# Column and row tiles for the fifth mixing input, two-pass scaled rows and a new order in a software-pipelined RWKV kernel

## The chip, the cores and the metric

The kernel runs on one core of one Trainium2 chip. The metric is the device time of one execution in microseconds, lower is better. A core has TensorE (PE, with its weight loads shown as PEld), VectorE (DVE), ScalarE (ACT), GpSimd (POOL) and SyncE (SP, which issues DMAs here). Each engine works through its own list in order, and they meet only in semaphores.

## The reference, cut to what matters

Input x is 2 x 4096 x 256, f32. It is an adaLN block: `h = layernorm(x) * (1 + ca) + sa`, then `x = x + ga * rwkv(h)`, then `h = layernorm(x) * (1 + cb) + sb` and `x = x + gb * ffn(h)`. The six modulation rows come from a small product and are one row of 256 for each batch.

rwkv has two layers and a last layernorm (`ln_out`). A layer is a time mixing and a channel mixing. What the change touches of the time mixing:

```python
sx  = shift(x) - x                              # x is the layer's layernorm
mix = tanh((x + sx * x_maa) @ tm_w1)            # 256 -> 160 = 5 groups of 32
m_f = mix[:, f] @ tm_w2[f]                      # five products 32 -> 256: w, k, v, r, g
f_x = x + sx * (f_maa + m_f)                    # then x @ Wr, Wk, Wv, Wg, and the decay from the w input
```

A recurrence over time (state times decay plus k v), a group norm, a gate and `@ Wo` follow. The ffn quantizes its input, its hidden values and its weights to blockwise FP4 (blocks of 16) and is `silu(gate) * up` with 704 hidden values, then a product down.

## The kernel before, in words

The 4096 tokens are cut into 32 tiles of 128, and both batches of a tile (NC = 2) are worked together, so a tile is 256 tokens: 128 partitions x 512 values (2 batches x 256 features) token-first, or the same with features on partitions.

The work of a tile is cut into five streams: 0 and 1 are the time mixings of layers 0 and 1 (stream 0 also holds the input layernorm), 2 and 3 the channel mixings, 4 the output layernorm and the ffn. A stream is a list of stages (`schedule`). `ORDER` gives for each engine one turn of the pipeline: `0/1 mf.2 mf.4` means stages mf.2 and mf.4 of stream 0 for the tile one turn back. Every engine runs its turn again and again, over 32 tiles and four more turns to drain; stages of tiles that do not exist are left out. Semaphores carry the dependences.

The stages that matter here:

- `lna` makes the layernorm's statistics on DVE (two bn_stats, two bn_aggr, one add), and POOL makes `rstd` of them (L562). `lnb` normalizes in two DVE tensor_scalar passes, subtract mean and multiply by rstd (L886). Seven layernorms run for a tile: in, tm0, cm0, tm1, cm1, out and ffn.
- `h0`, `x2` and `hf` follow the in, out and ffn layernorms: DVE multiplies by a modulation row in one 128x512 pass (L891), then POOL adds the shift row or the residual (L566, L628, L632).
- `turn` transposes rows to columns on PE (L1077), ACT moves them to hT (L684, L687), POOL makes sx (L572).
- `mix`: DVE makes the input (L906), PE multiplies by tm_w1: 128 columns into one half of a PSUM bank (L1109), the last 32 columns over all 256 tokens into the other (L1111); ACT takes tanh of both (L694, L695).
- `mf.0` to `mf.4`: five products of 32 rows (L1122), DVE adds maa and multiplies by sx (L918, two passes each), POOL adds x (L585). mf.0 to mf.3 read partitions 0 to 127 of the first tanh by quarters, mf.4 reads partitions 96 to 127 of the second, with the weights tm_w2b there.
- `pw1` (L1130), `pk`, `pr`, `pg` (L1085), `pv`, `wo` (L1093), `pw2` (L1164) are projections; ACT makes the decay of pw2 (L727, L731), and POOL multiplies it up over six levels (`tot`, L593).
- `lev.1` to `lev.6`: PE makes scores in small tiles (L1183, L1190), DVE scales r and k (L952) and merges scores under a mask (L954, L959). Each level's products on PE wait until DVE has emptied the previous level's two banks.
- `kt`, `st`, `ov`, `gna`, `gnb`, `yt`: transposes, states, outputs, group norm and gate. `ck`, `cr`, `cv` (L1267, L1093, L1281) are the channel mixing, `xt`, `gu`, `ht`, `dn` (L1077, L1300, L1311, L1319) the ffn, `qa` and `qc` its quantizing on DVE (L394 to L419).

Streams 0 and 1 have three PSUM banks each, A, B and C (`MIX_PSUM`); streams 2 to 4 share two, used alternately in PE's order. `fill` on PE waits until the last user of each bank has emptied it.

SP works through DVE's order: at stream 0's `wo` it waits until DVE has emptied that bank and loads the next x tile into xin (L496), at `x2` it loads x again for the residual (L500), at `dn` it waits for POOL's last add and stores (L504). In the first turns some setup hangs on names of places: the FP4 quantizing of the three ffn weights on DVE (`weights_norm`, `weights_grid`), on ACT and on PE.

Of the kernel before, what the change touches and what calls it, by code (L numbers as in the profile page):

```python
# [12 lines left out]
P = 128  # L13
# [19 lines left out]
    DVE: """0/1 mix; 4/4 qa.x; 2/2 cv; 4/4 qc.x; 1/3 st.0; 0/1 mf.0 mf.1; 1/3 st.1 gna; 4/4 gu.0.0; 0/1 mf.3; 1/3 gnb; 4/4  # L33
        gu.0.1 qa.0; 0/1 mf.2 mf.4; 1/3 wo; 4/4 qc.0; 1/2 lna.tm; 3/3 lna.cm; 0/1 lev.1; 1/2 lnb.tm; 4/4 gu.1.0; 0/1 lev.2;
        3/3 lnb.cm; 4/4 gu.1.1; 1/2 mix; 0/1 lev.3; 3/3 cmix; 0/1 pg lev.4; 1/2 mf.0; 0/1 lev.5; 1/2 mf.1 mf.3; 4/4 qa.1;
        0/1 lev.6; 4/4 qc.1; 1/2 mf.2; 0/1 st.0 st.1 gna; 1/2 mf.4; 0/1 gnb; 3/3 cv; 4/4 dn; 1/2 lev.1; 0/1 wo; 2/1 lna.cm;
        1/2 lev.2; 2/1 lnb.cm; 4/3 lna.out; 1/2 lev.3; 0/0 lna.in; 2/1 cmix; 0/0 lnb.in; 1/2 pg; 0/0 h0; 1/2 lev.4; 4/3
        lnb.out; 0/0 lna.tm; 4/3 x2; 1/2 lev.5; 0/0 lnb.tm; 4/3 lna.ffn; 1/2 lev.6; 4/3 lnb.ffn hf""",
    AC: """0/1 yt; 1/2 pv; 2/1 turn.cm; 1/2 pg; 2/1 ck.0 ck.1 ck.2 cr; 0/0 turn.tm; 1/2 kt; 4/3 qa.x; 0/0 mix; 4/3 xt; 1/2 gna;
        4/3 gu.0.0; 0/0 pw1; 4/3 gu.0.1; 0/0 pk; 1/2 yt; 4/3 qa.0; 0/0 pr pw2; 4/3 ht.0 gu.1.0; 0/0 pv; 1/1 turn.tm; 4/3  # L40
        gu.1.1; 3/2 turn.cm; 0/0 pg; 1/1 mix; 3/2 ck.0; 1/1 pw1; 4/3 qa.1; 3/2 ck.1; 1/1 pk; 0/0 kt; 3/2 ck.2 cr; 4/3 ht.1;
        1/1 pr; 0/0 gna; 1/1 pw2""",
    POOL: """3/3 cv; 1/2 mf.4; 0/1 yt; 1/2 tot; 2/1 lna.cm; 4/4 dn; 2/1 cmix; 0/0 lna.in; 4/3 lna.out; 0/0 h0 lna.tm; 4/3 x2
        lna.ffn; 0/0 mix; 4/3 hf; 1/2 st.0 st.1; 0/0 mf.0 mf.1; 1/2 gnb; 0/0 mf.3; 2/1 cv; 1/2 yt; 0/0 mf.2; 1/1 lna.tm; 3/2
        lna.cm; 0/0 mf.4 tot; 1/1 mix; 3/2 cmix; 1/1 mf.0 mf.1 mf.3; 0/0 st.0 st.1; 1/1 mf.2; 0/0 gnb""",
# [37 lines left out]
def orders(streams):  # L83
# [25 lines left out]
    "h_scaled": (["h0", "hf"], 1), "h_done": (["h0", "hf"], 1), "x2_scaled": (["x2"], 1), "x2_done": (["x2"], 1),  # L109
# [12 lines left out]
def adaln_rwkv_fp4_kernel(nc, a, out):  # L122
# [74 lines left out]
    with ExitStack() as ctx:  # L197
# [322 lines left out]
        def _(pool):  # L520
# [43 lines left out]
            def h0(i, b, _):  # L564
                after(pool, i, "h_scaled", b, "h0", 0)
                pool.tensor_tensor(xin[:, :, :], xn[b][:, :, :], rows[:, :, 0, :], ALU.add)\  # L566
                    .then_inc(ev["h_done"][b], 1)

# [55 lines left out]
            def x2_(i, b, _):  # L624
                pool.wait_ge(x_loaded_again, i * 16 + 16)
                pool.wait_ge(stored, i * 16 + 16)
                after(pool, i, "x2_scaled", b, "x2", 0)
                pool.tensor_tensor(x2[:, :, :], xagain, xn[b][:, :, :], ALU.add).then_inc(ev["x2_done"][b], 1)  # L628

            def hf(i, b, _):  # L630
                after(pool, i, "h_scaled", b, "hf", 0)
                pool.tensor_tensor(xn[b][:, :, :], xn[b][:, :, :], rows[:, :, 3, :], ALU.add)\  # L632
                    .then_inc(ev["h_done"][b], 1)
# [716 lines left out]
```

## Time and profile before

| what | value |
|---|---|
| median of 3 runs | 3316.56 us (3314.88 to 3319.21) |
| the profiled execution's own time | 3318.94 us |
| its span | 3317.2 us |
| granted TensorE clock over the span | 0.957 |
| busy: PE, PEld | 2986.0 us (90%), 2328.5 us (70%) |
| busy: DVE, POOL, ACT | 2413.7 us (73%), 1398.4 us (42%), 1269.9 us (38%) |
| DMA | 41.43 MB, mean 12 GB/s |

Busy is the time in which an engine has an instruction running; overlapping instructions count once. A clock of 1.00 is 2.4 GHz, 0.5 is 1.2 GHz. A line number names the line of the kernel that issued an instruction.

### The profile page before, as it was taken

The page shows a single profiled execution, that of the slowest core. Times are in us where ns is not written, and L with a number is a line of the kernel's source. Part 1 is how long each engine was busy: PE and PEld are TensorE (multiplying, and loading weights), DVE is VectorE, ACT ScalarE, POOL GpSimd, SP SyncE. Part 2 cuts the span into 40 slices and gives each one's busy share as a digit, 9 for nine tenths or more (in the row PEclk, how much of TensorE's full clock was granted, in tenths as well). Part 3 has the DMA queues.
Part 4 walks back from the last instruction along what each step waited for, and adds up shares of the span by engine and source line. Part 5 has one row for each costly group of instructions (what it writes and reads, how often), then busy time and mean ns, then how long its engine had stood idle before and what let it go on. Part 6 is the DMA issues. An engine that isn't in the chain of part 4 may idle for free.

```text
span 3317.2 us, 78375 instructions
## 1 busy us (share of the span) xinstructions
PE 2986.0 (90%) x32829; PEld 2328.5 (70%) x32829; DVE 2413.7 (73%) x5249; ACT 1269.9 (38%) x2451; POOL 1398.4 (42%) x1552
## 2 busy tenths in 40 slices
...
DMA packets 36212, 41.43 MB, mean 12 GB/s; under 512 B 2716, under 2 KB 34584, under 8 KB 35864
## 3 DMA queue, kind: packets, MB, share of 16 engines
...
q14 instruction: 84, 0.69, 0.1%
...
## 4 chain that ended last, share of the span: by engine, by line
PE 55%; DVE 32%; issue 5%; POOL 4%; DMA 3%; ACT 1%; SPq 0%; DVEq 0%; ACTq 0%; POOLq 0%
PE ps_all L1085 9%; PE ps_all L1267 9%; PE ps_all L1281 6%; PE ps_all L1300 5%; PE ps_all L1319 5%; PE ps_all L1093 4%; DVE stats L874 4%; DVE sxrk L952 3%; PE ps_all L1122 3%; PE ps_all L1190 3%; DMA xin<-in_L_attn_x_dram 3%; PE ps_all L1077 2%; DVE att L959 2%; DVE mixin L886 2%; DVE xn_ffn L886 2%
## 5 line engine op out<-in xcount | busy, mean ns | idle before, releaser
L585 POOL TENSOR_TENSOR mixin<-mixin,hT_tm 128x512 f32<-128x512 f32 x320 | 387.6, 1221 | 295.9 <-DVE mixin L918 295.9
L1267 PE MATMUL ps_all<-chan,cwk 128*128 128x256 f32 x1536 | 389.5, 407 | 44.4 <-DVE chan L906 44.4
L562 POOL TENSOR_TENSOR rstd<-var,powc 128x2 f32<-128x2 f32 x224 | 206.0, 922 | 503.7 <-DVE var L880 503.4
L918 DVE SCALAR_TENSOR_TENSOR mixin<-ps_all,vcol,sxrk 128x256 f32<-128x256 f32 x640 | 270.4, 477 | 192.4 <-PE ps_all L1122 191.4
L1267 PEld LDWEIGHTS ps_all<-chan,cwk 128*128 128x128 f32 x1536 | 299.5, 201 | 92.5 <-issue 48.0
L1281 PE MATMUL ps_all<-cwv,chan 128*128 128x256 f32 x1536 | 346.8, 382 | 0.5 <-ACT ffn_work L763 0.5
L1190 PEld LDWEIGHTS ps_all<-sxrk 64*64 64x64 f32 x12288 | 220.2, 136 | 175.0 <-issue 174.9
L952 DVE TENSOR_TENSOR sxrk<-sxrk,dec 128x512 f32<-128x512 f32 x384 | 271.7, 708 | 63.2 <-PE ps_all L1190 59.0
L1190 PE MATMUL ps_all<-sxrk 64*64 64x32 f32 x12288 | 258.0, 222 | 64.9 <-DVE att L959 64.7
L1281 PEld LDWEIGHTS ps_all<-cwv,chan 128*128 128x128 f32 x1536 | 287.7, 191 | 39.9 <-ACT ffn_work L763 1.1
L604 POOL TENSOR_TENSOR lora<-S,dec 128x256 f32<-128x256 f32 x128 | 84.2, 658 | 429.2 <-DVE S L967 429.1
L704 ACT ACTIVATE tok<-ps_all 128x512 f32<-128x512 f32 x128 | 76.3, 596 | 434.3 <-PE ps_all L1093 265.6
L959 DVE COPY_PREDICATED att<-masks,ps_all 128x256 f32<-128x256 uint8 x384 | 203.3, 529 | 9.7 <-DVE att L954 0.5
L1300 PE MATMUL ps_all<-gateT,ffn_work 128*128 128x352 f32 x512 | 188.8, 492 | 15.1 <-ACT ffn_work L763 14.4
L736 ACT ACTIVATE chan<-ps_all 128x512 f32<-128x512 f32 x192 | 113.9, 593 | 206.4 <-PE ps_all L1267 206.4
L1300 PE MATMUL ps_all<-upT,ffn_work 128*128 128x352 f32 x512 | 175.6, 466 | 0.0
L1319 PE MATMUL ps_all<-downT,ffn_work 128*128 128x256 f32 x768 | 173.3, 383 | 0.7 <-ACT ffn_work L767 0.7
L1319 PEld LDWEIGHTS ps_all<-downT,ffn_work 128*128 128x128 f32 x768 | 145.0, 192 | 20.0 <-ACT ffn_work L767 1.1
L1020 DVE TENSOR_TENSOR xn_ffn<-ps_all,rows 128x512 f32<-128x512 f32 x32 | 22.1, 692 | 183.5 <-PE ps_all L1319 183.5
L593 POOL TENSOR_TENSOR dec<-dec 128x256 f32<-128x256 f32 (+5 forms) x384 | 141.2, 368 | 26.5 <-ACT dec L731 1.5
L1122 PE MATMUL ps_all<-lora,tm_w2a 32*128 32x256 f32 x1024 | 146.7, 403 | 1.9 <-ACT lora L695 1.9
L609 POOL TENSOR_TENSOR grstd<-gvar,powc 128x8 f32<-128x8 f32 x64 | 105.4, 1648 | 99.7 <-DVE gvar L974 96.6
...
## 6 DMA issues: line engine op xcount, KB each, us to landing
...
```

What stands on the lines that cost most here:

```text
L562: pool.tensor_tensor(rstd[b][:, :], var[b][:, :], powc[:, 0:NC], ALU.pow).then_inc(ev["ln_rstd"][b], 1)
L585: pool.tensor_tensor(m, m, hT["tm", l][:, :, :, 1:P + 1].rearrange("p k c t -> p (k c) t"), ALU.add).then_inc(ev["mixed"][b], 1)
L918: ins = v.scalar_tensor_tensor(mixes(b, f)[:, k, :], bank(b, "mf", lf, "m")[:, k * TT:(k + 1) * TT], col(f"{MIXES[f]}_maa", l, k), sx[b][: ...
L952: v.tensor_tensor(rko, rko, t, ALU.mult).then_inc(ev["rk_lev"][b], 1)
L959: v.copy_predicated(odd, mask, data).then_inc(free_of(b, "lev", lj, "a"), 1)
L1085: ins = pe.matmul(bank(b, kind, arg, use)[:, m * TT:(m + 1) * TT], w[:, k, m * P:(m + 1) * P], x[:, k, :], start=(k == 0), stop=(k == KC - 1))
L1122: ins = pe.matmul(bank(b, "mf", lf, "m")[:, k * TT:(k + 1) * TT], w[:, k * P:(k + 1) * P], x, start=True, stop=True)
L1190: ins = pe.matmul(bank(b, "lev", lj, "a", e)[q * HH:(q + 1) * HH, n:n + HH // 2].rearrange("p (n h) -> p n h", h=half), kk[b][p, k, t], od ...
L1267: ins = pe.matmul(bank(b, "ck", lj, "k")[:, m * TT:(m + 1) * TT], cwk[:, l, k, n:n + P], k_in[:, k, :], start=(k == 0), stop=(k == KC - 1))
L1281: ins = pe.matmul(bank(b, "cv", l, "v")[:, c * D:(c + 1) * D], relu[t // 2][:, t % 2, c * P:(c + 1) * P], cwv[:, l, t, :], start=(t == 0), ...
L1300: ins = pe.matmul(bank(b, "gu", cu, use)[:, 0:IH], xqT[:, k, c * P:(c + 1) * P], w[:, k, u * IH:(u + 1) * IH], start=(k == 0), stop=(k == ...
L1319: ins = pe.matmul(bank(b, "dn", 0, "o")[:, c * D:(c + 1) * D], hqT[:, j, c * P:(c + 1) * P], downT[:, j, :], start=(j == 0), stop=(j == IT ...
```

## The change

1. The last 32 mixing columns: the product of L1111 is made for each batch by itself, 128 tokens, batch 0 into partitions 0 to 31 and batch 1 into 32 to 63, that is on two column tiles of PE. Four matmuls of 128 columns stand where two of 256 stood. Its tanh is one ACT pass of 64x128 where it was 32x256.
2. mf.4 reads these two row ranges: for each half of the features and each batch one matmul on row tile 0 or 32, each batch into a bank of its own (A and B). The weights lie in both row ranges, by one more DMA per layer. mf.4 stands ahead of mf.2 in the stream, and mf.2 uses bank C where it used A.
3. Layernorms in, out and ffn: `lnb` makes `(x - mean) * row` in two scalar_tensor_tensor passes and no longer waits for rstd; `h0`, `x2`, `hf` are two DVE scalar_tensor_tensor passes, `* rstd + shift`. The three POOL adds of 128x512 are gone, and DVE itself waits for the second load of x and for the store.
4. ORDER of all four engines is another, and so are the places of the weights' setup.

```diff
 ORDER = {
-    PE: """0/1 mf.2 mf.4; 1/3 wo; 0/1 pw2 lev.1 pv; 4/4 ht.0 gu.1.0; 0/1 lev.2; 1/2 turn.tm; 4/4 gu.1.1; 0/1 lev.3; 3/3
-        turn.cm; 0/1 pg; 1/2 mix; 0/1 lev.4; 3/3 ck.0; 1/2 mf.0 mf.1 mf.3; 0/1 lev.5; 3/3 ck.1; 0/1 lev.6; 3/3 ck.2; 1/2 pw1
-        pk pr; 0/1 kt; 3/3 cr; 1/2 mf.2 mf.4; 0/1 st.0 ov.0; 4/4 ht.1; 0/1 ov.1 st.1; 3/3 cv; 1/2 pw2; 0/1 yt; 4/4 dn; 1/2
-        lev.1; 0/1 wo; 1/2 pv lev.2 lev.3; 2/1 turn.cm; 1/2 pg lev.4; 2/1 ck.0 ck.1 ck.2; 1/2 lev.5; 2/1 cr; 1/2 lev.6; 0/0
-        turn.tm; 2/1 cv; 1/2 kt; 0/0 mix; 1/2 st.0 ov.0; 0/0 mf.0 mf.1 mf.3; 4/3 xt; 1/2 ov.1 st.1; 4/3 gu.0.0; 0/0 pw1; 4/3
-        gu.0.1; 0/0 pk; 1/2 yt; 0/0 pr""",
...
+    PE: """1/3 ov.0; 0/1 pw1; 1/3 ov.1 st.1; 2/2 cv; 1/3 yt; 0/1 pk pr; 1/3 wo; 4/4 xt; 0/1 mf.4 mf.2; 4/4 gu.0.0; 0/1 pw2
+        lev.1 pv; 3/3 turn.cm; 0/1 lev.2; 4/4 gu.0.1; 1/2 turn.tm; 0/1 lev.3 pg; 3/3 ck.0; 0/1 lev.4; 3/3 ck.1 ck.2 cr; 0/1
+        lev.5; 1/2 mix; 4/4 ht.0; 0/1 lev.6; 4/4 gu.1.0; 0/1 kt; 1/2 mf.0 mf.1 mf.3; 0/1 st.0 ov.0; 4/4 gu.1.1; 0/1 ov.1
+        st.1; 3/3 cv; 1/2 pw1; 0/1 yt; 1/2 pk pr; 0/1 wo; 1/2 mf.4 mf.2; 4/4 ht.1; 1/2 pw2; 4/4 dn; 1/2 lev.1 pv lev.2; 2/1
+        turn.cm; 0/0 turn.tm; 1/2 lev.3 pg lev.4; 2/1 ck.0 ck.1; 1/2 lev.5; 2/1 ck.2; 0/0 mix; 1/2 lev.6; 0/0 mf.0 mf.1
+        mf.3; 1/2 kt; 2/1 cr; 1/2 st.0""",
+    DVE: """4/4 gu.0.1; 0/1 lev.3; 4/4 qa.0; 0/1 pg lev.4; 1/2 mix; 4/4 qc.0; 0/1 lev.5 lev.6; 4/4 gu.1.0; 1/2 mf.0; 0/1 st.0;
+        1/2 mf.1; 4/4 gu.1.1; 1/2 mf.3; 0/1 st.1 gna; 4/4 qa.1; 0/1 gnb; 4/4 qc.1; 3/3 cv; 0/1 wo; 1/2 mf.4 mf.2; 2/1
+        lna.cm; 0/0 lna.in lnb.in; 2/1 lnb.cm; 0/0 h0 lna.tm; 1/2 lev.1; 0/0 lnb.tm; 1/2 lev.2; 4/4 dn; 1/2 lev.3; 2/1 cmix;
+        1/2 pg lev.4; 0/0 mix; 1/2 lev.5; 4/3 lna.out; 1/2 lev.6; 0/0 mf.0 mf.1; 4/3 lnb.out x2; 1/2 st.0; 0/0 mf.3; 4/3
+        lna.ffn lnb.ffn; 1/2 st.1 gna; 4/3 hf; 1/2 gnb; 4/3 qa.x qc.x; 2/1 cv; 1/2 wo; 0/0 mf.4; 3/2 lna.cm; 0/0 mf.2; 1/1
+        lna.tm; 3/2 lnb.cm; 4/3 gu.0.0; 0/0 lev.1; 1/1 lnb.tm; 0/0 lev.2; 3/2 cmix""",
+    AC: """0/1 pv; 1/2 turn.tm; 3/3 ck.0; 0/1 pg; 4/4 qa.0; 3/3 ck.1 ck.2 cr; 4/4 ht.0; 1/2 mix; 0/1 kt; 4/4 gu.1.0 gu.1.1; 0/1
+        gna; 4/4 qa.1; 0/1 yt; 1/2 pw1 pk pr; 4/4 ht.1; 1/2 pw2 pv; 2/1 turn.cm; 1/2 pg; 0/0 turn.tm; 2/1 ck.0 ck.1; 0/0
+        mix; 2/1 ck.2; 1/2 kt gna; 0/0 pw1; 2/1 cr; 1/2 yt; 4/3 qa.x; 0/0 pk pr; 4/3 xt gu.0.0; 0/0 pw2; 3/2 turn.cm; 4/3
+        gu.0.1""",
+    POOL: """1/3 yt; 2/2 cv; 0/1 mf.4; 3/3 lna.cm; 0/1 mf.2; 1/2 lna.tm; 0/1 tot; 3/3 cmix; 1/2 mix; 0/1 st.0; 1/2 mf.0; 0/1
+        st.1; 1/2 mf.1 mf.3; 0/1 gnb yt; 3/3 cv; 1/2 mf.4 mf.2; 2/1 lna.cm; 0/0 lna.in lna.tm; 1/2 tot; 2/1 cmix; 0/0 mix;
+        4/4 dn; 0/0 mf.0; 4/3 lna.out; 1/2 st.0 st.1; 4/3 lna.ffn; 0/0 mf.1; 1/2 gnb; 0/0 mf.3""",
 }
...
-            ("pk", "k"): "B", ("pr", "r"): "C", ("mf.2", "m"): "A", ("mf.4", "m"): "B", ("pw2", "w"): "BC", ("lev.1", "a"): "AB",
+            ("pk", "k"): "B", ("pr", "r"): "C", ("mf.4", "m"): "AB", ("mf.2", "m"): "C", ("pw2", "w"): "BC", ("lev.1", "a"): "AB",
...
-                act.activation(lora[b][P - E:P, 1, :], m[P - E:P, TT:2 * TT], ACT.Tanh).then_inc(free_of(b, "mix", l, "m"), 1)
+                act.activation(lora[b][0:NC * E, 1, 0:P], m[0:NC * E, TT:TT + P], ACT.Tanh).then_inc(free_of(b, "mix", l, "m"), 1)
...
                 elif at == (0, "2 cmix"):
                     weights_norm(1)
+                elif at == (0, "2 cv"):
                     weights_grid(1)
                     weights_norm(2)
+                elif at == (0, "1 lna.tm"):
                     weights_grid(2)
...
             def lnb(i, b, s):
                 src = ln_source(i, s)
+                scaled = {"in": 1, "out": 2, "ffn": 4}
+                if s in scaled:
+                    if s == "out" and i > 0:
+                        after(v, i - 1, "y_done", FFN, "dn", 0)
+                    for c in range(NC):
+                        v.scalar_tensor_tensor(xn[b][:, c, :], src[:, c, :], mv[b][:, c, 0:1], rows[:, c, scaled[s], :], ALU.subtract, ALU.mult)\
+                            .then_inc(ev["ln_xn"][b], 1)
+                    return
                 after(v, i, "ln_rstd", b, "lna", s)
...
-            def scale_rows(i, b, s, n, event):
+            def shift_rows(i, b, s, dst, shift, event):
+                after(v, i, "ln_rstd", b, "lna", s)
                 after(v, i, "ln_xn", b, "lnb", s)
-                v.tensor_tensor(xn[b][:, :, :], xn[b][:, :, :], rows[:, :, n, :], ALU.mult)\
-                    .then_inc(ev[event][b], 1)
+                for c in range(NC):
+                    v.scalar_tensor_tensor(dst[:, c, :], xn[b][:, c, :], rstd[b][:, c:c + 1], shift[:, c, :], ALU.mult, ALU.add)\
+                        .then_inc(ev[event][b], 1)
...
             def x2_(i, b, _):
-                scale_rows(i, b, "out", 2, "x2_scaled")
+                v.wait_ge(x_loaded_again, i * 16 + 16)
+                v.wait_ge(stored, i * 16 + 16)
+                shift_rows(i, b, "out", x2, xagain, "x2_done")
...
                 for k in range(KC):
-                    ins = pe.matmul(m[P - E:P, TT:2 * TT], tm_w1[:, l, k, P:P + E], mixes(b, 4)[:, k, :], start=(k == 0), stop=(k == KC - 1))
+                    for c in range(NC):
+                        ins = pe.matmul(m[c * E:(c + 1) * E, TT:TT + P], tm_w1[:, l, k, P:P + E], mixes(b, 4)[:, k, c * P:(c + 1) * P],
+                                        start=(k == 0), stop=(k == KC - 1))
...
+                    else:
+                        for c in range(NC):
+                            ins = pe.matmul(bank(b, "mf", lf, "m", c)[:, k * P:(k + 1) * P], tm_w2b[c * E:(c + 1) * E, l, k * P:(k + 1) * P],
+                                            lora[b][c * E:(c + 1) * E, 1, 0:P], start=True, stop=True)
```

On ACT, the setup's third `weights_abs` moves from behind `2 ck.2` to the head of layer 1's first `turn`. The order before of DVE, ACT and POOL is in the code above.

## Rows read from the trace of the kernel before

**Rows 1.** The page: busy time and share of the span by engine.
```profile
PE 2986.0 (90%) x32829; PEld 2328.5 (70%) x32829; DVE 2413.7 (73%) x5249; ACT 1269.9 (38%) x2451; POOL 1398.4 (42%) x1552
```

**Rows 2.** Windows: length, busy time by engine (instructions), granted clock, DMA share, GB/s.
```profile
0.00:120.00 120.00, 63.10 (x489) 43.52 (x489) 64.87 (x125) 22.98 (x39) 31.73 (x70) 0.73 0.33 101
...
500.00:1000.00 500.00, 470.45 (x5280) 367.23 (x5280) 384.40 (x842) 201.55 (x391) 224.64 (x242) 0.98 0.03 9
```

**Rows 3.** DVE's L886 and L906, steady turns: least/median/longest ns, first to last start.
```profile
L886 DVE TENSOR_SCALAR xn_ffn<-x,mv,rstd x54: 401/628/1224, 399.8 to 2922.8; 128x256 f32<-128x256 f32 x54
L906 DVE SCALAR_TENSOR_TENSOR mixin<-sxrk,vcol,hT_tm x108: 477/479/1500, 401.9 to 2959.1; 128x256 f32<-128x256 f32 x108
```

**Rows 4.** PE's timeline in one turn: start, us, operation, records [idle before, releaser].
```profile
1958.44 1.05 PE L1111 MATMUL ps_all<-mixin,tm_w 128*32 128x256 f32 x4
1959.42 0.62 PE L1218 MATMUL ps_all<-tok 64*64 64x64 f32 x13
...
1966.61 0.66 PE L1130 MATMUL ps_all<-mixin,td_w 128*64 128x128 f32 x8
1967.19 1.45 PE L1300 MATMUL ps_all<-gateT,ffn_work 128*128 128x352 f32 x4
...
1973.65 0.48 PE L1122 MATMUL ps_all<-lora,tm_w2a 32*128 32x256 f32 x1
1973.66 0.48 PE L1122 MATMUL ps_all<-lora,tm_w2b 32*128 32x256 f32 x1
...
1974.72 1.99 PE L1093 MATMUL ps_all<-wo,mixin 128*128 128x256 f32 x8
...
1978.35 0.69 PE L1183 MATMUL ps_all<-mixin,sxrk 64*64 64x64 f32 x32 [0.99 <-issue]
...
1990.23 1.89 PE L1085 MATMUL ps_all<-mixin,wg 128*128 128x256 f32 x8
```

**Rows 5.** PE's timeline about 50 us later.
```profile
2032.24 0.73 PE L1190 MATMUL ps_all<-sxrk 64*64 64x32 f32 x32 [1.61 <-DVE att L959]
...
2034.16 2.87 PE L1085 MATMUL ps_all<-mixin,wg 128*128 128x256 f32 x8
```

**Rows 6.** ACT's timeline: the decay's first passes in that turn.
```profile
1977.41 0.84 ACT L727 ACTIVATE tok<-ps_all,vcol 128x256 f32<-128x256 f32 x2 [0.72 <-PE ps_all L1164]
```

**Rows 7.** DVE's timeline: two layernorms' statistics, and a level 1 from its first pass on.
```profile
1980.08 0.74 DVE L874 BATCH_NORM_STATS2 stats<-hand 128x6 f32<-128x256 f32 x2
...
1981.33 0.74 DVE L874 BATCH_NORM_STATS2 stats<-xres 128x6 f32<-128x256 f32 x2
...
2026.52 0.70 DVE L952 TENSOR_TENSOR sxrk<-sxrk,dec 128x512 f32<-128x512 f32 x1 [0.47 <-PE ps_all L1190]
...
2028.53 0.72 DVE L987 TENSOR_TENSOR xres<-xin,ps_all 128x512 f32<-128x512 f32 x1
```

**Rows 8.** Groups by line: busy us, mean ns | idle before, releaser.
```profile
L566 POOL TENSOR_TENSOR xin<-mixin,rows 128x512 f32<-128x512 f32 x32 | 52.2, 1631 | 74.0 <-DVE mixin L891 74.0
...
L632 POOL TENSOR_TENSOR xn_ffn<-xn_ffn,rows 128x512 f32<-128x512 f32 x32 | 45.7, 1428 | 42.1 <-DVE xn_ffn L891 42.1
...
L891 DVE TENSOR_TENSOR xn_ffn<-xn_ffn,rows 128x512 f32<-128x512 f32 x64 | 44.1, 689 | 1.2
...
L628 POOL TENSOR_TENSOR x<-tok,xn_ffn 128x512 f32<-128x512 f32 x32 | 40.9, 1278 | 11.6 <-DVE xn_ffn L891 11.6
```

**Rows 9.** SP's timeline, then the landing times of L496's 31 loads.
```profile
2032.68 0.38 SPq L504 DMA_DIRECT2D out_dram<-x  x1
2033.11 0.47 SPq L496 DMA_DIRECT2D xin<-in_L_attn_x_dram  x1
...
DMA to landing us min/median/max: 2.6/2.9/4.3
```

**Rows 10.** PE's timeline in the first turns and in the last.
```profile
131.36 1.08 PE L1077 MATMUL ps_all<-ident,mixin 128*128 128x128 f32 x4 [19.21 <-DVE mixin L886]
...
3270.76 1.09 PE L1077 MATMUL ps_all<-ident,ffn_work 128*128 128x128 f32 x4 [16.07 <-DVE ffn_work L419]
```

More of the change, by code:

```diff
@@ L33 @@
[L33 to L45, printed above, removed]
+    PE: """1/3 ov.0; 0/1 pw1; 1/3 ov.1 st.1; 2/2 cv; 1/3 yt; 0/1 pk pr; 1/3 wo; 4/4 xt; 0/1 mf.4 mf.2; 4/4 gu.0.0; 0/1 pw2
[4 more added lines that the diff above has]
+        mf.3; 1/2 kt; 2/1 cr; 1/2 st.0""",
@@ L54, in schedule @@
         s += [("mf", (l, f)) for f in (0, 1, 3)]
-        s += [("pw1", l), ("pk", l), ("pr", l), ("mf", (l, 2)), ("mf", (l, 4)), ("pw2", l), ("tot", l)]
+        s += [("pw1", l), ("pk", l), ("pr", l), ("mf", (l, 4)), ("mf", (l, 2)), ("pw2", l), ("tot", l)]
         between = {1: ("pv", l), 3: ("pg", l)}
@@ L108 @@
     "ln_stats": (["lna"], 2), "ln_mv": (["lna"], 2), "ln_var": (["lna"], 1), "ln_rstd": (["lna"], 1), "ln_xn": (["lnb"], 2),
[L109 removed]
+    "h_done": (["h0", "hf"], 2), "x2_done": (["x2"], 2),
     "carried": (["turn"], 1), "shifted": (["mix", "cmix"], 1), "xxx": (["mix"], 1), "mixed": (["mf"], 1),
@@ L562, in lna @@
                 pool.tensor_tensor(rstd[b][:, :], var[b][:, :], powc[:, 0:NC], ALU.pow).then_inc(ev["ln_rstd"][b], 1)
[L564 to L567, printed above, removed]
             def shift(i, b, kind, l, stage):
@@ L622, in cv @@
                 pool.tensor_tensor(flat(hands(i, l)), flat(xres[l]), cm_r, ALU.add).then_inc(ev["cm_done"][b], 1)
[L624 to L633, printed above, removed]
             def dn(i, b, _):
@@ L637, in dn @@
                 pool.tensor_tensor(x2[:, :, :], x2[:, :, :], xn[b][:, :, :], ALU.add).then_inc(ev["y_done"][b], 1)
-            steps = {"lna": lna, "h0": h0, "mix": mix, "cmix": cmix, "mf": mf, "tot": tot, "st": st, "gnb": gnb, "yt": yt,
-                     "cv": cv, "x2": x2_, "hf": hf, "dn": dn}
+            steps = {"lna": lna, "mix": mix, "cmix": cmix, "mf": mf, "tot": tot, "st": st, "gnb": gnb, "yt": yt,
+                     "cv": cv, "dn": dn}
             turns(pool, RUN[POOL], steps, nothing)
@@ L682, in turn @@
                 h = hT[kind, l]
+                if (i, s) == (0, "tm1"):
+                    weights_abs(2)
                 filled(act, i, b, "turn", s, "x")
```

22 lines of the change are left out of this document (12 added, 10 removed).

## The prediction, on record before the changed kernel ran

> **What bounds the kernel now.** I read the page's busy shares first. PE is busy for 90% of the span, DVE for 73%, POOL and ACT for 42% and 38% [rows 1]. The windows say where the missing tenth is: in a steady window PE is busy for 470.45 of 500 us at a clock of 0.98, in the first 120 us for 63.10 at 0.73 [rows 2]. So there is a steady part, bound by PE and the waits in its list, and two ends, bound by chains of latency.
>
> The length of a steady turn comes from the first and last start of a group that runs twice a tile: 399.8 to 2922.8 us over 26 turns is 97.0 us [rows 3]. PE is busy for 94.1% of it, 91.3 us, and idle for 5.7 us. The clock's mean of 0.98 means about 2% of 97 us, 1.9 us, of full-speed work lost per turn. PE's timeline shows both. A level of batch-merged scores waits 1.61 us for DVE, and just behind it the gate's projection takes 2.87 us at the lower clock, where the same one takes 1.89 us elsewhere [rows 4, 5]. Another wait is 0.99 us before lev.1, marked "issue" [rows 4]. The code tells what it is: lev.1 uses banks A and B, pw2 used B and C, and ACT reads pw2 from 1977.41 for 0.84 us [rows 6], up to 0.1 us before lev.1 starts. The timeline's idle marks of one turn add up to 5.3 us at nine places; the largest are these two.
>
> What counts is therefore PE's work per turn, its waits in the new list, the clock, and the ends.
>
> **The fifth mixing input on PE.** Four records of 256 columns on one column tile last from 1958.44 to 1959.42, 0.98 us. The nearest row for the new form is pw1: eight records of 128 columns on two column tiles of 64, from 1966.61 to 1967.19, 0.58 us [rows 4]. Eight in a row without overlap would take 0.98 us again, so pw1 shows real overlap. I take 0.58: 0.40 saved per layer, 0.8 us per turn. Bounds: nothing saved, or 1.0 us per turn if tiles of 32 columns, with their shorter weight loads, overlap wholly. The smaller tanh (64x128 where it was 32x256) I cost at nothing; it lies on the way from mix to mf.0, 0.1 us.
>
> The Trainium skill (TensorEngine Tiling (Array Packing), Instruction Overhead) gives about 60 cycles of overhead to each matmul and advises against taking the factor from a dimension that is already small. By it the four more records cost an estimated 0.1 us per mix, some 6 us in all. The same page (Key Properties) says that changing the tiling mode drains the engine; the old product was already in a 128x32 mode, so no drain is added.
>
> **mf.4 on row tiles.** This saves PE nothing. mf.2 and mf.4 already run side by side: they start at 1973.65 and 1973.66 and both are done when wo starts at 1974.72, 1.07 us for both [rows 4]. mf.2 still has four records of 256 columns, and these fill that time. What mf.4's shorter product gives is a start for DVE about half a microsecond sooner. What it costs is banks: mf.4 holds A and B and mf.2 holds C, so pw2 (B, C) now waits for DVE's passes of both. I bound the pair by 0.9 and 1.3 us.
>
> **Rows in two DVE passes.** Before, a scaled layernorm is two tensor_scalar and one 128x512 multiply of 0.69 us, then a POOL add of 1.63, 1.28 or 1.43 us [rows 8]. The tensor_scalar passes run from 401 to 1224 ns [rows 3]. After, it is four scalar_tensor_tensor of 479 ns, 1.92 us, against 2 x 0.63 + 0.69 = 1.95 us by the medians: even on DVE, between a gain of 1.2 and a loss of 0.4 us for each if they run undisturbed. A pass of that kind can be as long as 1500 ns [rows 3]. POOL loses 4.3 us per turn. In the steady part that is off the path, since POOL is busy for 45% and PE never waits on these adds directly. At the ends the three adds are in series with everything: the last tile's ffn input comes with PE idle for 16.07 us [rows 10], and the first tile's start is a chain too. I take 4.3 us once.
>
> The long passes are explained by row and page together. The Trainium skill (SBUF — State Buffer, SBUF: two separate sides) states that DVE and GpSimd share one port pair under an exclusive lock, and that a DVE op with two SBUF inputs contends for it as well as one in a two-port mode. The rows agree so far: the longest pass is 0.82 us over the shortest, less than one POOL add. By that rule the new passes can be blocked like the old, with three fewer POOL adds to block them.
>
> **DMAs and queues.** One small load per layer is added at the start, among weights that nobody waits for then: nothing. The load of the next x tile stands in SP's list where DVE's `wo` of stream 0 is. Before, `dn` stands ahead of it, so it goes out at 2033.11 behind the store at 2032.68, though DVE's wo pass was at 2028.53 [rows 7, 9]. In the new order wo comes before dn, and the load goes at once. It lands in 2.9 us, at most 4.3. Until then DVE has mf.4, mf.2 and one set of statistics, 1.9 + 1.25 = 3.2 us, so this is hidden by a margin of 0.3 us, and at worst costs DVE 1.2 us. x2's new waits on DVE (second load, store, rstd) would hold st.0 and mf.3 behind them and so ov.1 and pr on PE. Store and load have more than ten microseconds by the order. rstd comes behind POOL's mf.0 add; I take 0.3 us for it, seen on PE at yt.
>
> **The new order.** I laid PE's new list out end to end with the old durations and looked for each stage at what it waits on. Most have microseconds to spare. These don't:
>
> - lev.1 of layer 0 stands right behind pw2 again: 0.99 us, as before.
> - lev.2 of layer 0. From the end of mf.4, DVE has mf.4 and mf.2 (four passes, 1.9), two sets of statistics (1.25 each, 1980.08 to 1981.33), one lnb (0.8 to 1.3), two gu passes (1.1, between those of 256 and 512 columns) and lev.1 (2.0, 2026.52 to 2028.53) [rows 3, 7]: 8.3 to 8.8 us. PE has the rest of mf.2 (0.5), gu.0.0 (2.6), pw2 (0.6), the 0.99, lev.1 (1.1), pv (1.8) and a transpose (0.5): 8.1 us. Stall 0.6.
> - pw2 of layer 1 follows mf.4, mf.2 and ht.1 only, while DVE needs its four passes: 0.3.
> - lev.2 and lev.3 of layer 1. DVE has mf.4 and mf.2 (1.9), three sets of statistics (3.75), lnb.in and h0 (1.9), lnb.cm (0.8 to 1.3) and lev.1 (2.0): 10.4 to 10.9 us. PE has 0.5 + 0.8 (ht.1) + 0.6 + 0.3 + 5.3 (dn) + 1.1 + 1.8 = 10.4 us: stall 0.3. Between lev.2 and lev.3 PE has 1.6 us (the level and two transposes), DVE an lnb and a level, 2.3 to 2.5: stall 0.8.
> - mf.0 behind mix with one level between them: 0.2; yt: 0.3.
> - small waits of 0.2 to 0.3 us as the old turn has them, and idle that no mark names: 1.4.
>
> Sum 4.9 us against 5.7: 0.8 saved. The 1.61 us and 0.30 us around turn.cm and the 0.47 us between ht.0 and gu.1.0 go, and 1.7 us in other places come. One spell of the lower clock per turn I leave as it is: 1.1 us of idle between lev.2 and lev.3 of layer 1 is close to what preceded it before.
>
> Work and waits together: 1.6 us per turn. With 32 tiles less three in which the pipeline fills, 29 turns: 46 us. The ends: 4.3 us from the adds. The setup's quantizing now holds DVE in three pieces where it held it once, with PE idle for 19.21 us [rows 10]. Each piece may hold PE or not, and a tile's path is a quarter of a turn longer in the new order. I take nothing, with 20 us either way. Sum: 3318.9 - 46 - 4.3 = 3268.6 for an execution like the profiled one; that one was 2.4 us over the median, so 3266 us. One can tell 0.2%, 6.6 us, from no change.
>
> **The rivals.**
> 1. Slower: DVE's list between mf.4 and lev.2 sets the turn. For it speaks that both stretches come out within 0.7 us of PE's work, and that every pass in them may be up to 1 us longer when it meets a POOL add [rows 3]. Against it, POOL has 4.3 us less. It decides when the two stretches are together 1.8 us later than laid out. With two disturbed passes in the first and one in the second, 2.5 us, the time is 3266 + 29 x 2.5 = 3339 us.
> 2. Same: the waits at lev.1 and lev.2 of layer 0, 0.99 and 0.6 us, lie close enough to bring a second low spell of the clock per turn: 29 x 1.9 = 55 us, 3321 us. Against it, the 0.99 us alone did not.
> 3. Faster: the stalls in layer 1 are too small for any low spell: 3266 - 55 = 3211 us.
> 4. The column tiles do not overlap at 32 columns, and the change doesn't do what it says on PE: 0.4 x 2 x 29 = 23 us back, 3289 us.
>
> **How the numbers follow.** My forecast has 0.58, rival 1 0.22, rival 2 0.09, rival 3 0.07, rival 4 0.04. Faster by over 0.2% is the forecast with rivals 3 and 4, 0.69; within it rival 2, 0.09; slower rival 1, 0.22. The range of 3205 to 3335 us takes in rivals 2 to 4, both bounds of the ends, and the milder part of rival 1.
>
> **What would show it.** In the profile after: the mix tail at about 0.58 us; mf.4 with mf.2 in 1.1 us; the steady turn at 95.4 us with PE idle 4.9 us; waits before lev.2 and lev.3 of layer 1 and lev.1 and lev.2 of layer 0; one low spell of the clock per turn; no POOL rows of L566, L628, L632. The prediction is wrong if a wait that I found covered, above all on ACT's or POOL's list, turns out over 1.5 us per turn, or if the new setup costs more than 20 us.

## The result, and the profile after

The changed kernel takes 3190.74 us in the median of four runs (3187.98 to 3192.47), the kernel before 3317.89 us beside it: 0.9616 of the time, 95% interval 0.9599 to 0.9633. The forecast was 3266 us, with 3205 to 3335 us as the range. The sign was right; the gain is 127 us where 51 were forecast, and the time lies 14 us below the range.

The page's busy shares, which answer to [rows 1]:

```profile
PE 2926.2 (92%) x33341; PEld 2317.9 (73%) x33341; DVE 2383.7 (75%) x5345; ACT 1252.3 (39%) x2451; POOL 1270.3 (40%) x1456
```

The windows after, with the columns of [rows 2]:

```profile
0.00:120.00 120.00, 68.70 (x539) 47.87 (x540) 62.26 (x136) 24.25 (x45) 35.35 (x74) 0.76 0.33 102
...
500.00:1000.00 500.00, 479.54 (x5582) 381.36 (x5581) 394.58 (x888) 212.35 (x416) 211.34 (x237) 1.00 0.03 10
```

PE is busy for 479.54 us of 500 where it was 470.45, at a clock of 1.00 where it was 0.98. The time of a turn is read from dn's one pass on DVE, of `after` (the changed kernel) and then of `before`: first and last start, 26 and 25 turns apart.

```profile
L1022 DVE TENSOR_TENSOR xn_ffn<-ps_all,rows x27: 711/716/718, 476.9 to 2888.3; 128x512 f32<-128x512 f32 x27
```

```profile
L1020 DVE TENSOR_TENSOR xn_ffn<-ps_all,rows x26: 691/692/693, 471.9 to 2896.4; 128x512 f32<-128x512 f32 x26
```

That is 92.75 us against 96.98, 4.23 us a turn; 29 turns make 123 of the 127 us. The other 4 us or so are left for the ends. All marks of idle time on PE in one turn of `after` (its timeline, as in [rows 4, 5]):

```profile
2040.62 0.71 PE L1173 MATMUL ps_all<-decay_h,td_w 64*128 64x128 f32 x8 [0.58 <-issue]
2050.57 0.67 PE L1199 MATMUL ps_all<-sxrk 64*64 64x32 f32 x32 [0.86 <-DVE att L961]
2052.84 0.67 PE L1199 MATMUL ps_all<-sxrk 64*64 64x32 f32 x32 [0.58 <-DVE att L961]
2070.17 0.69 PE L1252 MATMUL ps_all<-S,sxrk 64*64 64x64 f32 x32 [0.22 <-issue]
2076.99 0.63 PE L1079 MATMUL ps_all<-ident,mixin 128*128 128x128 f32 x4 [0.28 <-DVE mixin L980]
2088.66 0.69 PE L1192 MATMUL ps_all<-mixin,sxrk 64*64 64x64 f32 x32 [0.98 <-issue]
```

In order: pw2 of layer 1, its lev.2 and lev.3, ov.1, yt, and lev.1 of layer 0. Six marks, 3.5 us, where before there were nine with 5.3. The mixing products after:

```profile
1921.38 1.13 PE L1111 MATMUL ps_all<-mixin,tm_w 128*128 128x256 f32 x4
1922.44 0.63 PE L1114 MATMUL ps_all<-mixin,tm_w 128*32 128x128 f32 x8
1923.00 0.87 PE L1320 MATMUL ps_all<-ident,ffn_work 128*128 128x128 f32 x6
...
1945.41 0.38 PE L1130 MATMUL ps_all<-lora,tm_w2b 32*128 32x128 f32 x2
...
1946.50 0.87 PE L1320 MATMUL ps_all<-ident,ffn_work 128*128 128x128 f32 x6
```

The tail lasts from 1922.44 to 1923.00, 0.56 us against 0.98; mf.4 with mf.2 from 1945.41 to 1946.50, 1.09 us against 1.07.

By PE's account the 4.2 us are 0.8 us of tiles, 1.9 us of idle time (5.7 to 3.8) and about 1.5 us that is left for the clock. That says where the time lay, not what held it there. The experiments were made for that.

A low spell, below, is a stretch in which the granted clock was 0.5, that is 1.2 GHz. `before` has one in each of its 25 steady turns, `after` one in 26.

### The profile page after: what moved, and what is told of

Same layout as the page of the kernel before. It is cut to its first block, busy times and chain, and to the rows that moved or that the text cites. A ratio compares the mean times of both kernels' runs of the same rounds, so it can differ in the third digit from the quotient of the medians.

```text
span 3190.7 us, 79561 instructions
## 1 busy us (share of the span) xinstructions
PE 2926.2 (92%) x33341; PEld 2317.9 (73%) x33341; DVE 2383.7 (75%) x5345; ACT 1252.3 (39%) x2451; POOL 1270.3 (40%) x1456
## 4 chain that ended last, share of the span: by engine, by line
PE 67%; DVE 13%; issue 11%; POOL 7%; ACT 2%; DMA 0%; DVEq 0%; ACTq 0%; POOLq 0%
PE ps_all L1087 11%; PE ps_all L1309 10%; PE ps_all L1095 7%; PE ps_all L1276 6%; PE ps_all L1290 6%; PE ps_all L1199 6%; PE ps_all L1328 5%; PE ps_all L1079 3%; PE ps_all L1126 2%; DVE sxrk L954 2%; POOL grstd L605 2%; DVE att L961 2%; PE ps_all L1320 2%; PE ps_all L1173 1%; POOL sxrk L568 1%
## 5 line engine op out<-in xcount | busy, mean ns | idle before, releaser
L581 POOL TENSOR_TENSOR mixin<-mixin,hT_tm 128x512 f32<-128x512 f32 x320 | 375.6, 1179 | 912.4 <-DVE mixin L920 910.3
L954 DVE TENSOR_TENSOR sxrk<-sxrk,dec 128x512 f32<-128x512 f32 x384 | 301.7, 786 | 217.0 <-PE ps_all L1199 214.4
L1276 PE MATMUL ps_all<-chan,cwk 128*128 128x256 f32 x1536 | 362.7, 386 | 3.0 <-DVE ffn_work L1015 3.0
L1276 PEld LDWEIGHTS ps_all<-chan,cwk 128*128 128x128 f32 x1536 | 284.7, 190 | 42.7 <-DVE ffn_work L1015 3.8
L563 POOL TENSOR_TENSOR rstd<-var,powc 128x2 f32<-128x2 f32 x224 | 179.8, 803 | 201.5 <-DVE var L867 192.0
L589 POOL TENSOR_TENSOR dec<-dec 128x256 f32<-128x256 f32 (+5 forms) x384 | 150.3, 391 | 38.8 <-ACT dec L716 13.6
L610 POOL TENSOR_TENSOR mixin<-mixin,gg 128x512 f32<-128x512 f32 x64 | 82.9, 1296 | 194.9 <-ACT mixin L733 194.9
L733 ACT ACTIVATE mixin<-ps_all,vcol 128x256 f32<-128x256 f32 x128 | 65.2, 559 | 237.8 <-PE ps_all L1079 237.8
L1015 DVE TENSOR_TENSOR ffn_work<-ps_all,ffn_work 128x352 f32<-128x352 f32 x128 | 66.5, 519 | 120.6 <-ACT ffn_work L742 120.6
L568 POOL TENSOR_TENSOR sxrk<-hT_tm 128x512 f32<-128x512 f32 x64 | 79.9, 1248 | 190.4 <-ACT hT_tm L672 190.4
```

The source lines that it names most:

```text
L563: pool.tensor_tensor(rstd[b][:, :], var[b][:, :], powc[:, 0:NC], ALU.pow).then_inc(ev["ln_rstd"][b], 1)
L581: pool.tensor_tensor(m, m, hT["tm", l][:, :, :, 1:P + 1].rearrange("p k c t -> p (k c) t"), ALU.add).then_inc(ev["mixed"][b], 1)
L954: v.tensor_tensor(rko, rko, t, ALU.mult).then_inc(ev["rk_lev"][b], 1)
L1276: ins = pe.matmul(bank(b, "ck", lj, "k")[:, m * TT:(m + 1) * TT], cwk[:, l, k, n:n + P], k_in[:, k, :], start=(k == 0), stop=(k == KC - 1))
```

## The experiments

Ratios are to the kernel before on the same chip, where its median was 3316 to 3318 us; each time is a median. "Over after" is the difference to the 3190.74 us of the changed kernel.

**Parts left out of the changed kernel.** `no_tiles` puts back the fifth mixing input with its banks, all else as after:

```diff
-                    for c in range(NC):
-                        ins = pe.matmul(m[c * E:(c + 1) * E, TT:TT + P], tm_w1[:, l, k, P:P + E], mixes(b, 4)[:, k, c * P:(c + 1) * P],
+                    ins = pe.matmul(m[P - E:P, TT:2 * TT], tm_w1[:, l, k, P:P + E], mixes(b, 4)[:, k, :], ...
```

> The changed kernel with the fifth mixing input as before: two products of 256 columns on one column tile, mf.4 on partitions 96 to 127 in bank B, mf.2 in bank A. Theory A (the order brings most of the gain, the tiles only their own 0.8 us of PE work per turn): 3191 + 23 = 3214 us, clock still 1.00 in steady windows. Rival B (the shorter mix is what lets PE run at the full clock all turn): the low spells come back, 3191 + 23 + 53 = 3267 us.

3212.33 us, ratio 0.9694 (0.9676 to 0.9712), no low spell of the clock in the steady turns. The tiles are worth 21.6 us in this order, as expected, and the clock does not hang on them.

`no_rows` puts back the scaled rows: lnb by tensor_scalar with its wait for rstd, a DVE multiply, a POOL add. The three adds stand in POOL's order behind their statistics:

```diff
-        ... 0/0 lna.in lna.tm; 1/2 tot; ... 4/3 lna.out; 1/2 st.0 st.1; 4/3 lna.ffn; 0/0 mf.1; 1/2 gnb; ...
+        ... 0/0 lna.in h0 lna.tm; 1/2 tot; ... 4/3 lna.out x2; 1/2 st.0 st.1; 4/3 lna.ffn hf; 0/0 mf.1; 1/2 gnb; ...
```

> The changed kernel with scaled rows as before: tensor_scalar, one multiply of 128x512, and the three POOL adds, set into POOL's order behind their statistics. Theory A (rows matter at the ends only): 3191 + 4 = 3195 us, up to 3205. Rival C (POOL's 4.3 us less and DVE's undisturbed passes are what made the waits before lev.2 and lev.3 short): 1 to 2 us per turn more, 3220 to 3250 us.

3395.41 us, ratio 1.024 (1.0224 to 1.0256): 205 us over after, and slower than before. Neither theory had this size. `order_only`, with neither rows nor tiles:

> The kernel before with the new order of all engines and the setup's new places, and neither tiles nor rows. Theory A: 3191 + 23 + 4 = 3218 us. Rivals B and C: 3250 us or more.

3495.45 us, ratio 1.0542 (1.0523 to 1.0561). The order alone is 5% slower than the old one. It is an order for the new rows. The parts do not add up: without rows the tiles are worth 100 us in this order (`order_only` against `no_rows`), with rows 21.6. Why is not shown; the waits of PE for DVE before the levels and before yt are 3.6 and 2.3 us a turn in `order_only` and 2.1 and 1.1 in `no_rows`.

**What the rows do for the order.** Two kernels put back one property each. `rstd_wait` has only the wait of lnb for rstd:

```diff
                 if s in scaled:
+                    after(v, i, "ln_rstd", b, "lna", s)
```

> The changed kernel, where lnb of in, out and ffn waits for rstd again, and nothing else. Theory G (the new order stands on the rows' shorter chains): in and ffn have lnb right behind lna, so DVE stands about 1 us for POOL at each, and the first delays lev.2 and lev.3 of layer 1: 1 to 2 us per turn, 3191 + 45 = 3236 us. Rival H (only the POOL adds matter): 3195 us or less.

3257.35 us, ratio 0.9823 (0.9809 to 0.9838): 67 us over after. Its waits, 500 to 2500 us (us in total, times, longest), first of PE, then of DVE:

```profile
PE ps_all L1080 <- DVE mixin L981: 40.3, 21, 2.2
...
DVE xn_ffn L877 <- POOL rstd L563: 43.6, 44, 1.2
...
DVE mixin L877 <- POOL rstd L563: 17.0, 21, 0.8
```

DVE stands for rstd for 60.6 us in 21 turns, 2.9 us a turn (0.4 in `after`), and PE gets it back as a wait of 1.9 us before yt, whose group norm DVE reaches later (0.28 in `after`), and one of 1.1 us before ov.1 (0.22).

`pool_add` keeps the early lnb and gives the last step back to POOL: DVE multiplies by rstd, POOL adds in one pass, POOL's order as in `no_rows`.

```diff
-                    v.scalar_tensor_tensor(dst[:, c, :], xn[b][:, c, :], rstd[b][:, c:c + 1], shift[:, c, :], ALU.mult, ALU.add)
+                    v.tensor_scalar(xn[b][:, c, :], xn[b][:, c, :], rstd[b][:, c:c + 1], None, ALU.mult)
...
```

> The changed kernel, where the last step of the three scaled layernorms is a POOL add again: DVE multiplies by rstd in two tensor_scalar passes, POOL adds rows or x in one 128x512. Theory G: h0 has lna.tm right behind it and hf only gnb before qa.x, so DVE stands for most of 1.6 and 1.4 us, and POOL's st.0, mf.1 and gnb come later: 2 to 3 us per turn, 3191 + 70 = 3261 us. Rival: DVE's list has room, 3195 to 3205 us.

3340.7 us, ratio 1.0076 (1.0061 to 1.0091): 150 us over after, twice what was expected. DVE's waits say that it is POOL's list that is late:

```profile
DVE mixin L994 <- POOL grstd L610: 86.5, 21, 4.1
...
DVE S L983 <- POOL lora L605: 44.3, 21, 2.1
DVE stats L877 <- POOL xin L567: 27.5, 20, 1.4
```

In `after` DVE waits for grstd 25.1 us in 22 turns, 1.1 us each; here 4.1. In POOL's list the adds of x2 and hf stand ahead of st.0 and gnb. Another place in POOL's order might cost less; none was tried. The two parts give 67 + 150 = 217 us, `no_rows` 205.

**Parts alone in the old order.** `rows_only`:

> The kernel before with the rows in two DVE passes alone, old order without the three POOL adds. Theory A: the ends' 4 us, 3314 us, and within 5 us of it. Rival C (relief of POOL and of the shared passes shortens the waits): 3290 us or less.

3277.02 us, ratio 0.9876 (0.9859 to 0.9894): 39 us less than `before`, which refutes that rows matter at the ends only. PE's timeline of before, and then of `rows_only` at the same places:

```profile
2047.34 0.63 PE L1077 MATMUL ps_all<-ident,mixin 128*128 128x128 f32 x4 [0.44 <-DVE mixin L886]
...
2053.78 1.10 PE L1109 MATMUL ps_all<-mixin,tm_w 128*128 128x256 f32 x4 [0.20 <-DVE mixin L906]
...
2058.76 0.63 PE L1077 MATMUL ps_all<-ident,ffn_work 128*128 128x128 f32 x4 [0.28 <-DVE ffn_work L419]
```

```profile
2018.63 0.66 PE L1073 MATMUL ps_all<-ident,mixin 128*128 128x128 f32 x4
...
2024.74 1.03 PE L1105 MATMUL ps_all<-mixin,tm_w 128*128 128x256 f32 x4
...
2029.31 0.66 PE L1073 MATMUL ps_all<-ident,ffn_work 128*128 128x128 f32 x4
```

Three waits are gone: those of turn.tm and mix, which stand behind the in and tm0 layernorms, and that of xt, behind the ffn layernorm. Each looked like one more small wait. The three marks are 0.92 us of the 1.2 us a turn (turns of 95.75 us); no row shows the rest. Whether it is the missing POOL adds or the missing wait for rstd that does it here was not tried in the old order.

`tiles_only` needs a move: mf.2 in bank C waits for ACT's pr, which the old ACT order has behind ht.1, so pr stands earlier.

```diff
-        ... 1/1 pk; 0/0 kt; 3/2 ck.2 cr; 4/3 ht.1; 1/1 pr; 0/0 gna; 1/1 pw2
+        ... 1/1 pk; 0/0 kt; 1/1 pr; 3/2 ck.2 cr; 4/3 ht.1; 0/0 gna; 1/1 pw2
```

> The kernel before with the tiles alone. With mf.2 in bank C the old order needs ACT's pr of layer 1 ahead of its ck.2, cr and ht.1, so that is moved too. Theory A: 0.8 us less PE work a turn, 3318 - 23 = 3295 us. Rival (the column tiles gain nothing): 3318 us.

3333.02 us, ratio 1.0048 (1.0032 to 1.0063): slower. PE's waits hold a new one, mf.2 for ACT's pr, 0.8 us in each turn, and the wait before xt is 0.6 us where it was 0.28:

```profile
PE ps_all L1128 <- ACT sxrk L714: 16.4, 21, 0.8
PE ps_all L1081 <- DVE ffn_work L419: 12.6, 21, 0.6
```

The new banks, and the place of pr that they ask for, take back what the tiles give, in an order that was not made for them. `tiles_rows` is the whole change without its order, with pr moved in the same way:

> The kernel before with tiles and rows in the old order (ACT's pr moved as in the run with tiles alone), that is the change without its order. Theory A: 3318 - 27 = 3291 us, so that the order is worth 100 of the 127 us. Rival: 3240 us or less, the order a small part.

3281.89 us, ratio 0.989 (0.9871 to 0.9908). The order is worth another 91 us on top.

**The load behind the store.** In the old order I had seen that the x load goes out behind the store [rows 9] and costed it at nothing. DVE's timeline of `before`, just ahead of cmix and ck.0:

```profile
2036.08 0.75 DVE L874 BATCH_NORM_STATS2 stats<-xin 128x6 f32<-128x256 f32 x2 [0.74 <-DMA xin<-in_L_attn_x_dram]
```

`load_first` is the kernel before with the load ahead of the store:

```diff
                 if (kind, arg) == ("wo", 0) and i + 1 < N:
                     load(i + 1)
+                    while waiting:
+                        store(waiting.pop())
...
+                elif kind == "dn" and i < N - 4:
+                    waiting.append(i)
```

> The kernel before, with SP's load of the next x tile issued ahead of the store that stood before it in SP's list (the last four stores unchanged). Theory E (in the late stretch of the old turn DVE, not PE, sets the time: the load waits behind the store, DVE's lna.in waits 0.8 us a turn for it, and cmix and so ck.0 come behind): 0.5 to 0.84 us per turn less, 3316 - 20 = 3296 us. Rival F (that wait is hidden, PE sets the time there): 3316 us.

> The same with the rows in two DVE passes. Theory E: 3277 - 20 to 24 = 3255 us, so rows and load together give 60 us in the old order. Rival F: 3277 us.

`load_first` takes 3282.13 us, ratio 0.9894 (0.9878 to 0.9911), `rows_load_first` 3242.89 us, ratio 0.9779 (0.9764 to 0.9793). Both are faster than expected: the load is worth 34 us, in both kernels, and rows and load together 73 us. SP's timeline of `load_first`:

```profile
2003.86 0.37 SPq L496 DMA_DIRECT2D xin<-in_L_attn_x_dram  x1
2007.27 0.38 SPq L504 DMA_DIRECT2D out_dram<-x  x1
```

The load leaves 3.4 us ahead of the store. DVE's waits on xin, 0.8 us a turn in `before`, are gone here and in `after`, where SP's order does the same. The wait alone would be some 24 us in 29 turns; the next section has the rest.

**The clock.** `filled_wait` adds work to PE in the 1.61 us of [rows 5], in the kernel before:

```diff
+                if b == 1 and j == 3:
+                    fill(pe, i, b, "pg", l, "g")
+                    after(pe, i, "mixed", b, "mf", (l, 4))
+                    for _ in range(3):
+                        pe.matmul(bank(b, "pg", l, "g")[:, 0:TT], wg[:, l, 0, 0:P], mixes(b, 4)[:, 0, :], start=True, stop=True)
```

> The kernel before with three products of 256 columns (1.35 us) added on PE between lev.2 and lev.3 of layer 1, into the bank that pg overwrites next: PE works where it waited 1.61 us. No wait is shortened, 1.35 us of useless work is added per turn. Theory A (the low clock follows that wait and costs 1.8 us a turn): 3318 - 52 = 3266 us and clock 1.00. Rival D (the low clock is no cost of that wait): 3318 us or more.

3323.58 us, ratio 1.0021 (1.0011 to 1.0031). Low spells in the steady turns fell from 25 to 12, and the time did not fall. PE's timeline of one turn of `filled_wait` without a low spell:

```profile
2030.56 1.56 PE L1178 MATMUL ps_all<-mixin,wg 128*128 128x256 f32 x6
2032.09 0.67 PE L1195 MATMUL ps_all<-sxrk 64*64 64x32 f32 x32
...
2033.58 1.89 PE L1085 MATMUL ps_all<-mixin,wg 128*128 128x256 f32 x8
2035.40 0.67 PE L1195 MATMUL ps_all<-sxrk 64*64 64x32 f32 x32
2039.46 1.75 PE L1272 MATMUL ps_all<-chan,cwk 128*128 128x256 f32 x7 [3.39 <-DVE chan L906]
```

pg took 1.89 us where it took 2.87 [rows 5], and ck.0 waited for DVE's cmix the longer: 3.39 us in this turn, in which x also came late, and about 2 us in most others, against 0.73 behind the slow pg. What that is worth shows in the turns of `before` itself, for its low spells lie in two places. One turn has it on pg [rows 5], another on ck.0; PE's timeline of the two, from pg or ck.0 on:

```profile
2038.36 5.42 PE L1267 MATMUL ps_all<-chan,cwk 128*128 128x256 f32 x24 [0.73 <-DVE chan L906]
```

```profile
1161.31 1.89 PE L1085 MATMUL ps_all<-mixin,wg 128*128 128x256 f32 x8
...
1165.89 7.02 PE L1267 MATMUL ps_all<-chan,cwk 128*128 128x256 f32 x24 [2.09 <-DVE chan L906]
```

In both, ck.0 begins 18.4 us after dn's first record, because it waits for DVE either way. In the first the spell is over by then; in the second it falls on ck.0, whose records with those of ck.1 and ck.2 take 7.02 us for 5.42. Counted from one dn on PE to the next, the 15 turns of the first kind last 96.37 us in the median and the 10 of the second kind 97.49; DVE's wait for x is 0.5 to 0.9 us in all but one of the first and two of the second. In `filled_wait` the 13 turns without a spell last 96.22, and the 12 with one, all on ck.0 and half of them with x late as well, 98.5. So the spell on pg, beside DVE's chain, cost nothing, and the one on ck.0, at the end of that chain, cost about 1.1 us. The added work removed the spells that cost nothing.

This also bears on the load. `load_first` has 20 turns without a spell, 4 with one on pg and 1 on ck.0: 95.50, 95.50 and 96.92 us. Its 34 us are an estimated 24 us of DVE's wait and, by 10 turns in 25 at 1.1 us, some 13 us of spells on ck.0. Why the spells on pg became rare too, no run shows.

`lev_adjacent` is the changed kernel with lev.3 of layer 1 right behind lev.2:

```diff
-        ... 1/2 lev.1 pv lev.2; 2/1 turn.cm; 0/0 turn.tm; 1/2 lev.3 pg lev.4; ...
+        ... 1/2 lev.1 pv lev.2 lev.3; 2/1 turn.cm; 0/0 turn.tm; 1/2 pg lev.4; ...
```

> The changed kernel with lev.3 of layer 1 right behind lev.2, and the two transposes behind it, as in the order before. Theory A (idle close together brings the low clock, which costs 1.8 us a turn on top): the two transposes' 1.1 us no longer fill the wait, 1.1 x 29 = 32 us, and one low spell per turn comes back, 1.8 x 29 = 52 us: 3275 us. Rival D (the clock stays high): 3223 us.

3259.08 us, ratio 0.9827 (0.981 to 0.9844): 68 us over after, between the two forecasts and nearer to A. Low spells are back in 21 of 26 steady turns, behind the longer wait:

```profile
1999.31 0.67 PE L1199 MATMUL ps_all<-sxrk 64*64 64x32 f32 x32 [0.87 <-DVE att L961]
2001.58 1.07 PE L1199 MATMUL ps_all<-sxrk 64*64 64x32 f32 x32 [1.60 <-DVE att L961]
2002.58 1.11 PE L1079 MATMUL ps_all<-ident,chan 128*128 128x128 f32 x4
```

A turn is 2.25 us longer. 1.1 us are the two transposes, which filled the wait, so about 1.2 us are left for the clock. The kernel's own turns say the same: from dn to dn the 5 without a spell last 94.07 us in the median, the 21 with one 95.17.

**Less of DVE's list around layer 1's levels.** `later_statistics` moves the next tile's tm0 statistics and lnb behind lev.2 and lev.3 of layer 1 on DVE, with POOL's rstd and PE's transpose moved to fit:

```diff
-        ... 0/0 h0 lna.tm; 1/2 lev.1; 0/0 lnb.tm; 1/2 lev.2; 4/4 dn; 1/2 lev.3; ...
+        ... 0/0 h0; 1/2 lev.1 lev.2; 0/0 lna.tm; 1/2 lev.3; 0/0 lnb.tm; 4/4 dn; ...
```

> The changed kernel with DVE's lev.1 and lev.2 of layer 1 ahead of the next tile's tm0 statistics, its lnb behind lev.3, PE's turn of it behind lev.4, POOL's rstd of it behind tot. The waits before lev.2 (0.86 us) and lev.3 (0.58 us) of layer 1 are what is left of DVE's list there. If DVE's extra passes cause them: the first goes, the second becomes 0.8 us, 0.6 us a turn less, 3191 - 17 = 3174 us. If the level's own three passes cause them: 3191 us or more.

3235.56 us, ratio 0.9765 (0.9748 to 0.9781), 45 us over after. Its marks of idle time in that stretch:

```profile
1984.15 0.67 PE L1199 MATMUL ps_all<-sxrk 64*64 64x32 f32 x32 [0.56 <-DVE att L961]
1986.42 0.67 PE L1199 MATMUL ps_all<-sxrk 64*64 64x32 f32 x32 [1.01 <-DVE att L961]
1990.17 0.63 PE L1079 MATMUL ps_all<-ident,mixin 128*128 128x128 f32 x4 [0.56 <-DVE mixin L881]
1991.56 3.69 PE L1276 MATMUL ps_all<-chan,cwk 128*128 128x256 f32 x16 [0.76 <-DVE chan L905]
```

The waits at lev.2 and lev.3 stay, 1.57 us together where they were 1.44: the levels' own passes, with less on PE to cover them between lev.2 and lev.3. Two new ones come where the moved passes are late. The extra passes were not what held PE there; in `after` DVE itself waits for PE's scores before its level passes in that stretch, 0.92 and 0.45 us.

## Why the prediction was off, point by point

**Right.** The mix tail: 0.58 forecast, 0.56 measured; 23 us forecast for it in rival 4, 21.6 measured by `no_tiles`. The pair mf.4 with mf.2 saved PE nothing. The waits of the new order stood at places named, but for ov.1's 0.22: lev.1 of layer 0 0.98 (0.99 forecast), lev.2 and lev.3 of layer 1 0.86 and 0.58 (0.3 and 0.8), pw2 0.58 (0.3), yt 0.28 (0.3). The load of x landed in time. About 4 us are left for the ends, where 4.3 were forecast; whether they are the POOL adds, no run shows.

**Wrong, the rows, and with them the idle time.** This is the first step that failed. The prediction put the three POOL adds "off the path", since "PE never waits on these adds directly", and gave them 4.3 us at the ends. PE waits on them one step later, in turn.tm, mix and xt. `rows_only` measured 39 us for that term in the old order. I put 4.9 us of idle a turn, it was 3.8. The 1.4 us of small waits and unnamed idle were carried over from the old turn, and about 0.9 us of them were not there, as much as the marks of turn.tm, mix and xt. The 0.6 us at lev.2 of layer 0 and the 0.2 us at mf.0 were laid out from the new order and were not there either; pw2 of layer 1 and lev.2 with lev.3 took 0.6 us more than forecast.

**Wrong, the load.** The step on DMAs read the load's place correctly and then asked only what the new order would cost, not what the old one did cost. In the old order it was 34 us.

**Wrong, the clock.** "One spell of the lower clock per turn I leave as it is": in `after` there is one in all the steady turns. Rival 3 had this, at 0.07 and at a price of 55 us. Both parts need correcting. With a transpose pair between them, waits of 0.86 and 0.58 us brought no low spell; adjacent, the second then 1.60 us in one piece, they did (`lev_adjacent`). And the price was not 1.9 us in each turn of the kernel before: it was nothing on pg, in 15 turns of 25, and about 1.1 us on ck.0, in 10. In the new order, with PE setting the time, it is 1.1 to 1.2 us by `lev_adjacent`. The idle (1.1 us) and the clock (about 1.5 us of PE's busy time) are the 2.6 us by which a turn is shorter than the 95.4 forecast.

The clock's 1.5 us in PE's account and rows' and load's gains are therefore partly the same microseconds: shorten DVE's chain, and the slow spell that it covered must go too, or it comes to light.

**Rival 1** (DVE's list sets the new turn) was the likeliest slower case, and does not hold for the change as made. Without the rows the order is slower than the old one, as `order_only` and `no_rows` show, but no run shows that it is DVE's list between mf.4 and lev.2 that sets it. The new passes were hardly blocked: the medians of L876 and L888 are 473 to 480 ns in five of the six groups. In the sixth, out's lnb, half of the 52 passes take 471 to 474 ns and the other half 840 to 846 ns. The long ones begin while POOL's L581 add runs and end 0.28 us after it.

The rule that the prediction cites says that of a GpSimd op and a DVE op with two SBUF inputs the first to start has the shared ports until it ends (the Trainium skill, SBUF — State Buffer, SBUF: two separate sides). The long passes agree with it, at 0.37 us each. The short ones run beside POOL's L563, on 128x2 values, and are not held up; the rule does not explain that part.

Rival 2's second low spell behind lev.1 and lev.2 of layer 0 did not come.

**The shares.** In the old order the load gives 34 us and the rows 39, together 73. In the new one the tiles give 21.6. If these shares held side by side, some 32 of the 127 us would be left for the rest of the order, where fewer and shorter waits and the freed clock are not told apart. That is an account and not a measurement: the load was not put back in the new order, and rows and tiles are worth other amounts there (205 us, and 21.6 or 100).
